# Five of six GpSimd adds of probability chunks become accumulating DMAs in a gated cross-attention and FP4 feed-forward kernel

## What is computed

```
x = x + tanh(g_xattn) * xattn(layernorm(x), ctx)
      # q, k, v projections; softmax(q k^T / 8) v for 16 heads; @ Wo + bo
x = x + tanh(g_ffn) * ffn(layernorm(x))
      # fp4(h) @ fp4(w_down)^T, h = silu(gate) * up; gate, up = fp4(z) @ fp4(w)^T
```

## Time and profile before

| | us |
|---|---|
| median of 3 runs | 597.64 |
| lowest and highest | 597.33, 598.23 |
| the profiled execution | 598.33 |
| its span in the trace | 596.1 |
| granted TensorE clock, mean | 0.958 |
| POOL busy, of which L505 | 276.3, 186.5 |

### The profile page before, as it was taken

How to read it: one execution, slowest core, us unless ns; L and a number is a source line. 1 busy time by engine, 2 the same in 40 slices (tenths; PEclk the granted TensorE clock), 3 DMA queues, 4 the chain that set the end, 5 groups by cost and what they waited for, 6 DMA issues and landing times.

```text
span 596.1 us, 9833 instructions
## 1 busy us (share of the span) xinstructions
PE 543.8 (91%) x2841; PEld 335.7 (56%) x2841; DVE 476.7 (80%) x793; ACT 312.3 (52%) x723; POOL 276.3 (46%) x234
## 2 busy tenths in 40 slices
PE   5889999999999998999999998999999999999642
PEld 4655565666566554666466554665566565656331
DVE  2769875889977996889977995789977997787655
ACT  3434756575456645575456644566456745546211
POOL 4007344553828173553828173363827264456400
PEclk9779999999999999999999999999999999999675
DMA  8500000200020000200020000200020000000000
GB/s 158 99 1 1 1 1 0 52 2 1 1 58 2 0 2 9 50 0 0 1 56 1 0 0 9 50 0 0 1 56 1 0 0 5 1 1 1 1 3 3
DMA packets 27892, 9.31 MB, mean 16 GB/s; under 512 B 24016, under 2 KB 27600, under 8 KB 27856
## 3 DMA queue, kind: packets, MB, share of 16 engines
q1 hardware_dynamic: 27856, 8.92, 7.5%
HBM read 8.50 MB, written 0.41 MB: 15 GB/s over the span
## 4 chain that ended last, share of the span: by engine, by line
PE 59%; DVE 27%; issue 10%; ACT 2%; DMA 1%; DVEq 0%; POOL 0%; SPq 0%; POOLq 0%; ACTq 0%
PE attn L789 16%; PE scores L775 11%; PE ring L728 10%; DVE max L897 8%; PE scores L776 7%; PE ring L735 4%; PE ring L742 4%; DVE f_abs L362 3%; DVE f_abs L364 2%; DVE e_gate L860 2%; DVE acc_v L919 2%; PE ring L707 2%; DVE h_fp L366 1%; DVE z L871 1%; DVE rsum L904 1%
## 5 line engine op out<-in xcount | busy, mean ns | idle before, releaser
L634 ACT ACTIVATE probs<-scores 120x400 f32<-120x400 f32 (+1 forms) x384 | 190.0, 504 | 211.7 <-PE scores L776 209.1
L897 DVE TENSOR_REDUCE max<-ring 116x1 f32<-116x482 f32 (+1 forms) x336 | 204.7, 649 | 28.4 <-PE ring L728 24.1
L505 POOL TENSOR_TENSOR acc_p<-acc_p,probs 120x800 f32<-120x800 f32 x79 | 156.3, 1978 | 61.7 <-ACT probs L634 58.1
L789 PE MATMUL attn<-probs,ctx_n 120*64 120x400 f32 (+1 forms) x768 | 173.9, 532 | 0.0
L775 PE MATMUL scores<-q_hh,k_hl 128*120 128x400 f32 (+1 forms) x384 | 155.0, 404 | 1.2 <-DVE q_ls L899 1.2
L775 PEld LDWEIGHTS scores<-q_hh,k_hl 128*120 128x120 f32 (+1 forms) x384 | 70.9, 185 | 128.2 <-ACT probs L634 70.2
L776 PE MATMUL scores<-q_ls,k_h 71*120 71x400 f32 (+1 forms) x384 | 134.8, 351 | 0.0
L728 PE MATMUL ring<-k_hl,q_hh 128*116 128x482 f32 (+1 forms) x336 | 119.6, 409 | 12.4 <-DVE max L897 4.7
L776 PEld LDWEIGHTS scores<-q_ls,k_h 71*120 71x120 f32 (+1 forms) x384 | 71.6, 186 | 4.2
L728 PEld LDWEIGHTS ring<-k_hl,q_hh 128*116 128x116 f32 (+1 forms) x336 | 59.1, 182 | 25.7 <-DVE max L897 9.9
L789 PEld LDWEIGHTS attn<-probs,ctx_n 120*64 120x64 f32 (+1 forms) x768 | 38.3, 136 | 46.4 <-issue 34.3
(11 more groups left out here) (127 smaller groups left out, 526.9 us busy)
## 6 DMA issues: line engine op xcount, KB each, us to landing
ctx_n<-in_ctx SPq DMA_DIRECT2D x16, 360.0 KB
wq<-in_L_xattn_Wq SPq DMA_DIRECT2D x1, 512.0 KB, 4.6
wo<-in_L_xattn_Wo SPq DMA_DIRECT2D x1, 512.0 KB, 6.8
x_in<-in_x SPq DMA_DIRECT2D x8, 50.0 KB
out<-y_out SPq DMA_DIRECT2D x8, 50.0 KB
wk<-in_L_xattn_Wk SPq DMA_DIRECT2D x1, 256.0 KB, 4.1
ctx_n<-in_ctx SPq DMA_DIRECT2D x16, 1.0 KB
wv<-in_L_xattn_Wv SPq DMA_DIRECT2D x1, 256.0 KB, 6.3
```

Source lines behind the costliest of these rows:

```text
L505: pool.tensor_tensor(acc_p[0:r, t.g % 2, :], left, probs[0:r, c % PROBS, :], ALU.add).then_inc(sum_p, 1)
L634: act.activation(probs[0:r, c % PROBS, k * HALF:(k + 1) * HALF], scores[0:r, slot % SCORE_BANKS, 0:HALF], ACT.Exp).then_inc(probs_full, 1)
L789: mm = pe.matmul(attn[64 * i:64 * i + C, k, 0:HALF], ctx_n[0:r, par, c, 0, :], probs[0:r, c % PROBS, k * HALF:(k + 1) * HALF], start=(j == ...
L897: dve.tensor_reduce(max3[0:rows, tile, part:part + 1], src[0:rows, 0:MAXC[part + 1] - MAXC[part]], AX.X, ALU.max).then_inc(free, 1)
```

## The change

GpSimd keeps its first add of a group (chunks 1 and 2). Each of the other five (chunks 4, 5, 6, 7, 8) becomes a DMA that GpSimd issues with an add as its accumulation, from the chunk's buffer in `probs` onto `acc_p`. They are issued one at a time: before each one GpSimd waits until the one before has landed (`sum_d`, 16 counts each), and for the first one of a group for its own add as well. Between that wait and the DMA stands an add of one element on a small tile, `pause`. ACT, when it overwrites the buffer of such a chunk, and DVE, before `add_last`, wait for `sum_d` too. In the last group chunk 8 moves to DVE, which leaves three DMAs. `last_heads` waits for `head_done` in addition.

```diff
-ADDS_V, ADDS_P = len(SUM_V), len(SUM_P) - 1
+ADDS_V, ADDS_P = len(SUM_V), 1
-LAST_SUM_V, LAST_SUM_P = [0, 3, 6, 9, 10, 11], [1, 2, 4, 5, 7, 8]
+LAST_SUM_V, LAST_SUM_P = [0, 3, 6, 8, 9, 10, 11], [1, 2, 4, 5, 7]
+DMA_ADDS = len(SUM_P) - 2
...
+        pause = sb("pause", [1, CHUNKS])
...
+        def dma_adds(t, n, back=0):
+
+            return t.count(16 * DMA_ADDS, 16 * (n - DMA_ADDS * back))
...
-            own, per, done = (by_v, ADDS_V, sum_v) if c in by_v else (by_p, ADDS_P, sum_p)
-            return done, t.count(per, max(own.index(c), 1) - per * back)
+            if c in by_v:
+                return sum_v, t.count(ADDS_V, max(by_v.index(c), 1) - ADDS_V * back)
+            if c in by_p[:2]:
+                return sum_p, t.count(ADDS_P, 1 - ADDS_P * back)
+            return sum_d, dma_adds(t, by_p.index(c) - 1, back)
...
-                    left = probs[0:r, own[0], :]
+                    pool.tensor_tensor(acc_p[0:r, t.g % 2, :], probs[0:r, own[0], :], probs[0:r, c % PROBS, :], ALU.add).then_inc(sum_p, 1)
                 else:
-                    pool.wait_ge(sum_p, t.count(ADDS_P, i - 1))
-                    left = acc_p[0:r, t.g % 2, :]
-                pool.tensor_tensor(acc_p[0:r, t.g % 2, :], left, probs[0:r, c % PROBS, :], ALU.add).then_inc(sum_p, 1)
+                    if i == 2:
+                        pool.wait_ge(sum_p, t.count(ADDS_P, 1))
+                        if t.g >= 1:
+                            pool.wait_ge(sum_d, dma_adds(t, 0))
+                    else:
+                        pool.wait_ge(sum_d, dma_adds(t, i - 2))
+                    pool.tensor_tensor(pause[0:1, i:i + 1], pause[0:1, 0:1], pause[0:1, 0:1], ALU.add)
+                    pool.dma_start(acc_p[0:r, t.g % 2, :], probs[0:r, c % PROBS, :], accum_op=ALU.add).then_inc(sum_d, 16)
...
                 wait_reads(dve, (t, ("sum", 0)))
+                dve.wait_ge(head_done, t.count(4, -4))
...
-                dve.wait_ge(sum_p, own_adds(t, 1))
-                dve.wait_ge(sum_v, own_adds(t, 0))
+                dve.wait_ge(sum_d, dma_adds(t, len(chunks_of(t.g - 1)[1]) - 2, 1))
+                dve.wait_ge(sum_v, own_adds(t))
```

More of the change, by code:

```diff
@@ L275, in xattn_ffn @@
         sum_p = sem("sum_p")
+        sum_d = sem("sum_d")
         norm_done = sem("norm_done")
@@ L314, in chunks_of, with own_adds @@
             return (LAST_SUM_V, LAST_SUM_P) if g == GROUPS - 1 else (SUM_V, SUM_P)
-        def own_adds(t, which):
-            own = len(chunks_of(t.g - 1)[which]) - 1
-            return t.count((ADDS_V, ADDS_P)[which], own - (ADDS_V, ADDS_P)[which])
+        def own_adds(t):
+            return t.count(ADDS_V, len(chunks_of(t.g - 1)[0]) - 1 - ADDS_V)
+        def dma_adds(t, n, back=0):
+            return t.count(16 * DMA_ADDS, 16 * (n - DMA_ADDS * back))
         def added(t, c, back=0):
             by_v, by_p = chunks_of(t.g - back)
-            own, per, done = (by_v, ADDS_V, sum_v) if c in by_v else (by_p, ADDS_P, sum_p)
-            return done, t.count(per, max(own.index(c), 1) - per * back)
+            if c in by_v:
[3 more added lines that the diff above has]
+            return sum_d, dma_adds(t, by_p.index(c) - 1, back)
         def all_groups(engine, group, finish):
@@ L443, in _ @@
             pool.memset(ident[:, :], 0.0).then_inc(consts_set, 1)
+            pool.memset(pause[:, :], 0.0)
             pool.memset(ones[:, :], 1.0).then_inc(consts_set, 1)
@@ L732, in ring_use @@
                 elif kind == "sum":
-                    pe.wait_ge(sum_v, own_adds(t, 0) + 1)
+                    pe.wait_ge(sum_v, own_adds(t) + 1)
                     for h in range(HG):
```

## The result

The changed kernel takes 728.29 us (median; 727.11 to 730.44) against 597.93 us: 1.2185 times as long, with a 95% interval from 1.2157 to 1.2213. The forecast was 647.5 us, with 580 to 735 as its range: slower, as forecast, but by 130 us and not by 50.

What follows compares the result with a forecast made beforehand. The bound was the add_last cadence, 67.15 us a pair of groups. Ten 5.2 us links plus 21.0 make 73.0: +43.9 us over 7.5 pairs, +6 for context loads, on 598.3; less 0.7 for the median, 647.5 us, range 580 to 735.

Steps and rivals of the forecast that it cites:

- What bounds the kernel, and the deadline: Loop cadence closed by DVE's add_last, 67.15 us a pair of groups; anything arriving later than add_last wants it stretches this.
- Break-even at 4.6 us a link: GpSimd's transfer chain: about 4.6 us from one issue to the next fits the existing cadence.
- Part 1, the lifted contention: Without GpSimd's adds beside them DVE's L362, L364, L366 shorten: 2.4 us an odd group, at most 17 us, if transfers are in time.
- Part 2, the link: Time per chained transfer, including wait, one-element add and issue: taken as 5.2 us from bounds and nearby transfers.
- One bound: Link time estimated from the last store's issue and landing: 3.8 us with the second read, 4.4 with a 0.6 us issue.
- rival A: GpSimd's links are short, 3.8 to 4.4 us; add_last hardly waits and lifted contention shows: 583 us, chance 0.22.
- Part 4, the context loads: SP's context loads share DMA engines with chunk 8's transfer: 1.0 us in each of 6 even groups, +6 us.
- the tail of 21.0 us a pair: From add_last to the next group's first issue: 9.3 us in an even and 11.7 us in an odd group, kept unchanged.
- "0 to 24 us": PE's matmuls at a lower granted clock after idle time: up to 1.6 us a group over 15 groups, left to the range.
- this sign of being wrong: A time from add_last to the next first issue longer than 9.3 and 11.7 us would show the forecast wrong.
- rival B: GpSimd's links are long, 6.4 to 7 us, from held-up descriptors or slow DMA addition: 745 us at 6.5, chance 0.15.

Runs made afterwards that it cites:

- four_links: The changed kernel with chunk 8 added by DVE in every group, leaving four accumulating transfers a group: 641.87 us.
- no_links: The changed kernel without its accumulating DMAs, chunks 4 to 8 left out of the sum and only the one-element adds kept: 578.84 us.
- warm_pe: The changed kernel with extra matmuls, results unused, on PE where it stalls after a group's turn: 703.92 us.
- halves_four: The changed kernel with chunk 8 moved to DVE and each remaining accumulation split into two overlapping half-width DMAs: 591.86 us.

## Why the prediction was right in sign and wrong in size

- **What bounds the kernel, and the deadline: right in the main.** The kernel before was a cadence that any later arrival at add_last stretches; the landing became that arrival. ACT's exponential of chunk 2 waits for the same landing, and counting both once was right. Left out was that the landings before it hold ACT as well: chunk 7's held the exponential of chunk 1 and stalled PE for 2.04 us before the last wait began, and in `four_links` this deadline is the binding one.
- **Break-even at 4.6 us a link: borne out.** Links of 2.2, 3.7 and 3.75 us gave 579, 590 and 591 us, with nearly the same cadence in the loop; 5.45 gave 728.
- **Part 1, the lifted contention: right in mechanism, and near in size by luck.** The forecast was at most 17 us (581 us) if nothing waits for the transfers; `no_links` gave 578.8, 19.6 us less than the kernel before. But the loop gave 1.3 us a pair and not 2.4 (the head sum beside L365 takes 0.9 us of DVE back; that this is the difference is not shown), and the last two groups and what follows them gave 8.4 us that I had not looked for. That it would not help when add_last waits was right.
- **Part 2, the link: a little low, by errors that nearly cancel.** I took 5.2 us. Measured are 5.45 between ordinary issues and 5.68 as the mean of ten (27.90 us from 388.32 to 416.22 and 28.88 from 346.69 to 375.57, with a first link of 5.9 in each). Inside it, I gave about 3.0 us to what is fixed and 2.2 to the bytes, two reads at the rate of HBM loads; measured are 2.2 and 3.3. One bound was summed wrongly: with 0.6 us for the issue in place of 0.29, the 3.8 us become 4.1 and not 4.4, and the 0.6 is the issue of Wo in the trace (0.59 us), which no row shows. The ends of the range do not follow from the sum either: links of 4.6 and 6.3 us give 602 and 730 us by it, not 599 and 735. The page "DMA: Bandwidth & Descriptors" of the Trainium skill, section "Anatomy of one DMA", gives 2.0 us as fixed, and the 2.0 us landing of 16 columns agrees. Its 436 GB/s does not agree, since two passes at it are, as an estimate from that page, 1.76 us against 3.3, and one pass is 0.88 against the 1.6 of the copy. "Collectives: The Full Stack" of the Trainium skill, Part 3, says of a reduce in a collective that it pays a second read and not the addition; the factor of about two between adding and copying agrees with that, without showing which of the two it is. By these two rules rival A would have come true; it fell with the byte rate.
- **Part 4, the context loads: small.** The last link of group 7, beside them, was 6.57 us, 1.1 longer than its neighbours; I had counted 1.0.
- **The step that failed: the tail of 21.0 us a pair, taken over unchanged.** Counted with the links of groups 7 and 8 it is 84.06 - 56.8 = 27.3 us in the changed kernel (27.1 as the mean over the groups of the loop). In a pair, the links are 4.0 us more than forecast (56.8 against 52.0 and 0.8 for the loads), the tail 6.3 us: times 7.5, 30 and 47 us, and 647.5 + 77 = 725 us, near the 727.1 us of the profiled execution. I had seen the mechanism (0.95 against 1.00 in the earlier trace rows) and gave it "0 to 24 us" in the range and nothing in the sum, since I priced it from a window with 1.9 us of idle time, while my own forecast added 2.9 us of waiting to every group. `warm_pe` shows that the 12.75 us tail goes back to 9.31 once PE is kept busy through the stall. The sum is near by extrapolation: it puts 7.5 equal pairs for six pairs in the loop and longer first groups.
- **The prediction named this sign of being wrong**: "a tail longer than 9.3 and 11.7 us after add_last, which would mean that the second half of the loop is not what I took it for". That is what happened; the loop's second half is the same work, partly at half the clock.

So rival B's time came about without its cause: the links are 5.7 us on the mean and not 6.5, and the clock came on top.

## What to carry to other kernels

Work moved off a busy engine into a chain of transfers is priced per link, against the time until the earliest user of what the chain holds, and that includes the next writer of each buffer it reads, not only the reader of the result. What followed the work on its old engine now starts earlier, and can meet another engine's work there. When the sum says that a nearly full TensorE will stall for some microseconds in every round, put the clock's fall into the sum with the slowed matmuls after the stall, not into the range. And when a serial chain misses its deadline, shorten it or split it into chains that overlap before dropping it: three links (592.4 us) or half-width pairs with four chunks (591.9 us) both came in 1% under the original, which here was gained in the last groups and not in the loop.

## What the runs showed of the hardware that I had not expected

- An accumulating SBUF-to-SBUF transfer of 120 rows of 3200 B landed 5.4 us after its issue, a copy of the same bytes after 3.6, an accumulation of half the width after 3.5 and one of 64 B a row after 2.0. The queue's packets were 11232 for 78 accumulations, whatever their width, and 6240 for 78 copies.
- Issuing took GpSimd 0.76 us for an accumulation (median of 78) and 0.53 for a copy.
- DVE's L365 on 100x352 took 0.52 to 0.53 us with no GpSimd arithmetic beside it, 1.53 entirely beside GpSimd's head sum (six times in `no_links` and six in the changed kernel) and 2.13 beside the head sum and the end of an issue (six times in `halves_four`).
- Around the passage to group 8, PE was idle for 2.04 us, worked from 369.5, and its granted clock fell from 1.00 to 0.50 between 371 and 372; it was 1.00 again from 385, after PE had been idle for 3.28 us up to 376.04 and then busy for all but 0.4 us.
